# Softmax of the first attention: the negated maximum is added by VectorE from a broadcast tile instead of by a fourth product of TensorE

## What is computed

```python
q = _rmsnorm(hidden_states @ Wq_a, q_a_ln_w) @ Wq_b          # 32 heads, 128 + 64 wide
ckv = hidden_states @ Wkv_a
compressed, k_pe = (ckv[..., :KV_RANK], ckv[..., KV_RANK:])   # 64 and 64 wide
kv = _rmsnorm(compressed, kv_a_ln_w) @ Wkv_b
...
scores = jnp.einsum('bhqd,bhkd->bhqk', qf, kf) * scale
scores = jnp.where(causal, scores, jnp.finfo(scores.dtype).min)
probs = jax.nn.softmax(scores, axis=-1)
o = jnp.einsum('bhqk,bhkd->bhqd', probs, v)
return o.transpose(0, 2, 1, 3).reshape(b, s, H * VD) @ Wo
```

## Time and profile before

| | |
|---|---|
| three executions | 2632.04, 2634.44, 2639.09 us |
| profiled execution | 2627.89 us, its span 2626.1 us |
| mean granted clock of TensorE | 0.918 |
| TensorE busy, 12704 matmuls | 2225.0 us, 85% |
| VectorE busy | 1402.9 us, 53% |
| ScalarE busy | 1264.4 us, 48% |
| GpSimd busy | 629.5 us, 24% |
| stage of the 32 heads | about 205 to 858 us |

### The profile page before, as it was taken

How to read it: one execution, slowest core, us unless ns; L and a number is a source line. 1 busy time by engine, 2 the same in 40 slices (tenths; PEclk the granted TensorE clock), 3 DMA queues, 4 the chain that set the end, 5 groups by cost and what they waited for, 6 DMA issues and landing times. The chain is left out here.

```text
span 2626.1 us, 34151 instructions
## 1 busy us (share of the span) xinstructions
PE 2225.0 (85%) x12704; PEld 1310.7 (50%) x12704; DVE 1402.9 (53%) x1949; ACT 1264.4 (48%) x2113; POOL 629.5 (24%) x460
## 2 busy tenths in 40 slices
PE   4989999999999767759999957679999977998847
PEld 3657777777777653324444323234444333443434
DVE  3564555554554254559999654159999631113163
ACT  4545556655565232218888832118888841101330
POOL 1555555665566022400000022100000020001021
PEclk8989999999999888869999958879999998999868
DMA  4870111111110310331121001341121003000000
GB/s 102 260 223 25 53 52 52 56 44 52 52 53 32 109 35 21 107 68 20 20 38 20 2 17 53 125 70 23 28 48 28 2 17 129 0 0 5 14 27 34
DMA packets 78947, 138.97 MB, mean 53 GB/s; under 512 B 30808, under 2 KB 40792, under 8 KB 78832
## 3 DMA queue, kind: packets, MB, share of 16 engines
q1 hardware_dynamic: 78832, 137.40, 18.8%
HBM read 95.95 MB, written 41.03 MB: 52 GB/s over the span
## 5 line engine op out<-in xcount | busy, mean ns | idle before, releaser
L2159 POOL TENSOR_TENSOR l0a_p_low<-yT,l0a_p_high 128x1024 fp32r<-128x1024 f32 (+7 forms) x256 | 385.8, 1535 | 282.6 <-ACT l0a_p_high L2187 282.6
L173 POOL TENSOR_TENSOR applied<-prepared,neghalf 128x2 f32<-128x2 f32 x64 | 58.3, 911 | 1410.6 <-DVE prepared L154 1410.6
L1441 DVE TENSOR_REDUCE l2a_mx<-ps 128x2 f32<-128x1024 f32 x256 | 309.2, 1223 | 78.2 <-PE ps L1315 77.5
L1441 DVE TENSOR_REDUCE l1a_mx<-ps 128x2 f32<-128x1024 f32 x256 | 309.3, 1223 | 51.3 <-PE ps L1315 50.6
L2220 DVE TENSOR_REDUCE l0a_mx<-ps 128x1 f32<-128x512 f32 (+3 forms) x384 | 203.6, 554 | 235.9 <-PE ps L2066 145.0
L1422 ACT ACTIVATE l1a_prob<-ps 128x512 f32<-128x512 f32 x512 | 278.1, 596 | 75.2 <-PE ps L1343 58.6
L1422 ACT ACTIVATE l2a_prob<-ps 128x512 f32<-128x512 f32 x512 | 278.1, 596 | 68.6 <-PE ps L1343 50.6
L2176 ACT ACTIVATE yT<-ps 128x1024 f32<-128x1024 f32 (+7 forms) x256 | 166.2, 649 | 188.4 <-PE ps L2088 125.6
L2187 ACT CAST l0a_p_high<-yT 128x1024 fp32r<-128x1024 f32 (+7 forms) x256 | 172.7, 674 | 7.1
L191 ACT ACTIVATE f<-f,applied 128x512 f32<-128x512 f32 x64 | 48.6, 806 | 250.3 <-POOL applied L176 250.0
L1358 PE MATMUL ps<-l1a_prob,l1a_vext 128*32 128x256 f32 x2048 | 166.4, 405 | 0.0
(11 more groups left out here) (297 smaller groups left out, 4065.3 us busy)
## 6 DMA issues: line engine op xcount, KB each, us to landing
l0a_q<-l0a_q SPq DMA_DIRECT2D x32, 512.0 KB, 3.2
l0q_woh<-in_l0a_wo SPq DMA_DIRECT2D x16, 512.0 KB, 5.3
l0a_q<-f SPq DMA_DIRECT2D x32, 256.0 KB, 4.7
l0a_q<-l0q_q_pe SPq DMA_DIRECT2D x32, 256.0 KB, 3.5
l0a_recip_rows<-l0a_recip_row SPq DMA_DIRECT2D x32, 256.0 KB, 3.3
l0a_o<-l0a_o_pair SPq DMA_DIRECT2D x16, 512.0 KB, 2.8
yT<-l0a_o SPq DMA_DIRECT2D x16, 512.0 KB, 3.2
l1a_q<-l1a_q_parts SPq DMA_DIRECT2D x16, 256.0 KB, 5.3
```

The lines of the kernel that those rows point to most:

```text
L1441: nc.vector.tensor_reduce(mx[:, u % 2, :, p, t, c], banks(("pair", m)), AX.X, ALU.max).then_inc(s_red, 1)
L2159: nc.gpsimd.tensor_tensor(p_low[:, j % 4, P * j:T], prob[:, j % 4, P * j:T], p_high[:, j % 4, P * j:T], ALU.subtract).then_inc(s_pl, 1)
```

## The change

- `mrow`, `ones` and `diag` and their memsets and load are gone, and with them the fourth product of each part (L2086) and VectorE's multiply (L2225). `mcol` is 8 columns of fp32r instead of 128 of float32.
- `max_turn` makes eight products of 128 columns instead of one transpose: the weights are one column of `mcol`, broadcast to 128, and the moving operand is the identity; so every partition gets the negated maxima of all 1024 queries (`MAXIMA`, banks 6 and 7).
- ScalarE copies them to the tile `mrows` (128x1024, two buffers), behind step 4's cast. Chunk 0 of the head after waits for this copy.
- VectorE adds `mrows` to each score tile (`less_max`) and writes `prob`; ScalarE's exp reads and writes `prob`. TensorE waits for the addition of tile j (`s_less`) where it waited for the exp. The addition waits for its tile in PSUM, and for `p_high` and `p_low` of the tile that had the slot, which the exp's wait was before.
- VectorE's program is written anew, in steps like TensorE's: `invert` is in step 1, `negate` in step 2, `rest` in step 4, `finish` in step 5, and the additions stand between the reductions. In step 7 tile 1 of the next head is added before chunks 0 to 2 are reduced.
- On SyncE each `load` of a q comes after a `spread` instead of before it.

```diff
@@ -1725,11 +1725,10 @@
         def sb(n, shape, dt=F32):
             return mem.enter_context(nc.sbuf_tensor("l0a_" + n, shape, dt))
         self.q_high, self.q_low = sb("q_high", [P, 2, T], F32R), sb("q_low", [P, 2, T], F32R)
-        self.unit, self.mask, self.ones = sb("unit", [P, P], F32R), sb("mask", [P, P], F32R), sb("ones", [P, P], F32R)
+        self.unit, self.mask = sb("unit", [P, P], F32R), sb("mask", [P, P], F32R)
         self.c_high, self.c_low = sb("c_high", [P, NT, self.CV], F32R), sb("c_low", [P, NT, self.CV], F32R)
-        self.mrow = sb("mrow", [P, 2, T], F32R)
-        self.mx, self.mcol = sb("mx", [P, NT, 2]), sb("mcol0", [P, P])
-        self.diag = sb("diag", [NT, NT, P])
+        self.mrows = sb("mrows", [P, 2, T])
+        self.mx, self.mcol = sb("mx", [P, NT, 2]), sb("mcol0", [P, NT], F32R)
         self.mask16 = sb("mask16", [P, P], BF16)
 
 
...
     ST = [ps[:, 0:2, :].rearrange("p b n -> p (b n)"), ps[:, 2:4, :].rearrange("p b n -> p (b n)")]
     O = ps[:, 4:6, :].rearrange("p b n -> p (b n)")
+    MAXIMA = ps[:, 6:8, :].rearrange("p b n -> p (b n)")
     s_ph, s_pl = (chip.sem("l0h_" + n) for n in ("exps_high", "exps_low"))
     NH = MLA_HEADS
     OV = O[0:CV, :]
+
+    PLAN = [(3, 4, 5, 6), (6, 7, 8, 9), (9, 10, 11, 12)]
+    AHEAD = 3
 
     def bank(par, n):
         return ps[:, 6 + (par + n) % 2, :]
@@ -2025,15 +2023,15 @@
 
             load(2, 0, True)
             load(3, 1, True)
+            spread(0)
             load(4, 0)
-            spread(0)
             with sp.Fori(0, NH // 2 - 3) as i:
+                spread(i * 2 + 1)
                 load(i * 2 + 5, 1)
-                spread(i * 2 + 1)
+                spread(i * 2 + 2, i)
                 load(i * 2 + 6, 0)
-                spread(i * 2 + 2, i)
+            spread(NH - 5)
             load(NH - 1, 1)
-            spread(NH - 5)
             for h in range(NH - 4, NH):
                 spread(h, None if h % 2 else h // 2 - 1)
 
@@ -2052,12 +2050,9 @@
                     if not ready:
                         pe.wait_ge(s_high, h - 1)
                     if not first:
-                        pe.wait_ge(s_red, h * NMAX)
-                elif n == 1:
-                    if not first:
 
                         pe.wait_ge(s_mrow, h)
-                else:
+                elif n >= 2:
                     pe.wait_ge(s_red, h * NMAX + n - 1)
                 mm = nc.tensor.matmul(b[:, 0:width], q_high[:, par, qt * P:(qt + 1) * P],
                                       k_high[:, 512 * c:512 * c + width],
@@ -2068,22 +2063,22 @@
 
             def max_turn(h, par):
                 pe.wait_ge(s_neg, h + 1)
-                nc.tensor.transpose(bank(par, NMAX)[:, 0:P], mcol[:], chip.ident[:]).then_inc(s_mt, 1)
+                for t in range(NT):
+                    mm = nc.tensor.matmul(MAXIMA[:, t * P:(t + 1) * P], mcol[:, t:t + 1].broadcast_to([P, P]), unit[:],
+                                          start=True, stop=True)
+                mm.then_inc(s_mt, 1)
 
             def scores(h, par, j, ready=False):
 
-                if j == 0:
-                    pe.wait_ge(s_mrow, h + 1)
-                    if not ready:
-                        pe.wait_ge(s_low, h - 1)
+                if j == 0 and not ready:
+                    pe.wait_ge(s_low, h - 1)
                 for lo, hi in spans(j):
                     out = ST[j % 2][:, lo:hi]
                     diagonal = lo == P * j
                     keys = slice(j * P, (j + 1) * P)
                     nc.tensor.matmul(out, k_high[:, keys], q_high[:, par, lo:hi], start=True, stop=False)
                     nc.tensor.matmul(out, k_high[:, keys], q_low[:, par, lo:hi], start=False, stop=False)
-                    nc.tensor.matmul(out, k_low[:, keys], q_high[:, par, lo:hi], start=False, stop=False)
-                    mm = nc.tensor.matmul(out, ones[:], mrow[:, par, lo:hi], start=False, stop=not diagonal)
+                    mm = nc.tensor.matmul(out, k_low[:, keys], q_high[:, par, lo:hi], start=False, stop=not diagonal)
                     if diagonal:
                         mm = nc.tensor.matmul(ST[j % 2][:, lo:lo + P], mask[:], unit[:], start=False, stop=True)
                 mm.then_inc(s_st, 1)
@@ -2098,13 +2093,11 @@
                 mm.then_inc(s_pv, 1)
 
 
-            PLAN = [(3, 4, 5, 6), (6, 7, 8, 9), (9, 10, 11, 12)] + [(NMAX,) * 4] * 4
-            AHEAD = 3
             TURN_STEP = 3
 
             def head(h, par, first=False, last=False, no_second=False):
                 def chunks(j, part):
-                    if j < NT - 1 and not last:
+                    if j < len(PLAN) and not last:
                         for n in range(PLAN[j][part], PLAN[j][part + 1]):
                             max_chunk(h + 1, 1 - par, n)
                     if j == NT - 1 and not no_second:
@@ -2116,7 +2109,7 @@
                     if j == 0 and not first:
                         pv(h - 1, NT - 1)
 
-                    pe.wait_ge(s_exp, h * NT + j + 1)
+                    pe.wait_ge(s_less, h * NT + j + 1)
                     if j + 2 < NT:
                         scores(h, par, j + 2)
                     elif not last:
@@ -2167,13 +2160,14 @@
                 act.wait_ge(s_q[par], turn * 16 + 16)
                 nc.scalar.copy(q_high[:, par, :], q32[:, par, :]).then_inc(s_high, 1)
 
-            def head(h, par, next_turn, first, second=False):
+            def maxima(h, par):
+                act.wait_ge(s_mt, h + 1)
+                nc.scalar.copy(mrows[:, par, :], MAXIMA).then_inc(s_mrow, 1)
+
+            def head(h, par, next_turn, first, second=False, last=False):
                 for j in range(NT):
-                    act.wait_ge(s_st, h * NT + j + 1)
-                    if not (first and j < 4):
-
-                        act.wait_ge(s_pl, h * NT + j - 3)
-                    nc.scalar.activation(prob[:, j % 4, P * j:T], ST[j % 2][:, P * j:T], ACT.Exp,
+                    act.wait_ge(s_less, h * NT + j + 1)
+                    nc.scalar.activation(prob[:, j % 4, P * j:T], prob[:, j % 4, P * j:T], ACT.Exp,
                                          scale=SCALE).then_inc(s_exp, 1)
                     if j == 0 and not first:
                         if not second:
@@ -2185,6 +2179,8 @@
 
                         act.wait_ge(s_pv, h * NT + j - 3)
                     nc.scalar.copy(p_high[:, j % 4, P * j:T], prob[:, j % 4, P * j:T]).then_inc(s_ph, 1)
+                    if j == 4 and not last:
+                        maxima(h + 1, 1 - par)
                 if next_turn is not None:
 
                     cast(par, next_turn)
@@ -2194,13 +2190,14 @@
                 act.wait_ge(s_pv, h * NT + NT)
                 nc.scalar.copy(osum[:], O[0:KV_RANK + 1, :]).then_inc(s_os, 1)
 
+            maxima(0, 0)
             head(0, 0, 1, True)
             head(1, 1, 1, False, second=True)
             with act.Fori(1, NH // 2 - 1) as i:
                 head(i * 2, 0, i + 1, False)
                 head(i * 2 + 1, 1, i + 1, False)
             head(NH - 2, 0, None, False)
-            head(NH - 1, 1, None, False)
+            head(NH - 1, 1, None, False, last=True)
             act.wait_ge(s_on, NH - 1)
             lift(NH - 1)
 
@@ -2211,20 +2208,26 @@
                 nc.vector.tensor_tensor(q_low[:, par, :], q32[:, par, :], q_high[:, par, :],
                                         ALU.subtract).then_inc(s_low, 1)
 
-            def prepare(h, par, done=None):
-
-                for n, (qt, c, width, _) in enumerate(MAX_CHUNKS):
-                    if n == 6 and done is not None:
-                        invert(done)
-                    dve.wait_ge(s_mm, h * NMAX + n + 1)
-                    nc.vector.tensor_reduce(mx[:, qt, c:c + 1], bank(par, n)[:, 0:width], AX.X,
-                                            ALU.max).then_inc(s_red, 1)
+            def reduce_chunk(h, par, n):
+                qt, c, width, _ = MAX_CHUNKS[n]
+                dve.wait_ge(s_mm, h * NMAX + n + 1)
+                nc.vector.tensor_reduce(mx[:, qt, c:c + 1], bank(par, n)[:, 0:width], AX.X, ALU.max).then_inc(s_red, 1)
+
+            def negate(h):
                 dve.wait_ge(s_red, h * NMAX + NMAX)
-                nc.vector.tensor_reduce(mcol[:, 0:NT], mx[:], AX.X, ALU.max, negate=True).then_inc(s_neg, 1)
-                dve.wait_ge(s_mt, h + 1)
-                nc.vector.tensor_tensor(mrow[0:NT, par, :].rearrange("r (t q) -> r t q", t=NT),
-                                        bank(par, NMAX)[0:NT, 0:P].unsqueeze(1).broadcast_to([NT, NT, P]), diag[:],
-                                        ALU.mult).then_inc(s_mrow, 1)
+                nc.vector.tensor_reduce(mcol[:], mx[:], AX.X, ALU.max, negate=True).then_inc(s_neg, 1)
+
+            def less_max(h, par, j, first=False):
+
+                dve.wait_ge(s_st, h * NT + j + 1)
+                if j == 0:
+                    dve.wait_ge(s_mrow, h + 1)
+                if not (first and j < 4):
+
```

(64 more changed lines are left out.)

15 lines of the change are left out of this document (5 added, 10 removed).

## The result

The kernel after took 2661.38 us, the median of 5 runs (2654.84 to 2664.64); the kernel before took 2638.74 beside it (5 runs, 2632.04 to 2639.09). The ratio is 1.0087, with a 95% interval from 1.0066 to 1.0108: slower, by 0.9%. The profiled execution took 2661.96, with a span of 2659.9. In what follows one execution is out of line: one of e2's ten took 3053.44 us at a mean granted clock of 0.685, and e2's interval leaves it out.

A forecast was written before the change was run, and what follows sets the result against it. TensorE was the bound by busy sums, but waits on other engines were to decide: stretches 4.67 + 15.94 = 20.61 us per head against 20.33, +8.4 us over 30 heads, added to the median 2634.4 for 2643 us; range 2608 to 2672.

The forecast's parts named there:

- the waits eat what the products give: Main forecast: new TensorE waits on VectorE cancel the saved products, 0.28 us more per head, 2643 us; chance 0.50.
- The forecast's own range: 2631 to 2653 us, from other costs of the turn's products and overlapping VectorE starts.
- A: Stretch from the end of pv(h-1,7) to pv(h,0): two chains end together, so it stays 4.67 us.
- B: The rest of a head's period, from pv(h,0) to the end of pv(h,7): 15.66 us becomes 15.94.
- The twelve products: Fourth products removed from TensorE: 2.2 us per head, of which 0.35 + 0.35 lie in A.
- The baseline at the end of tile 1's products: In B, issue of tile 1's products ends 13.71 us after pv(h,0) before the change, 13.15 after it.
- Behind it: After tile 1's products: chunk 2 at 1.63 us, chunk 3 at 2.05, pv(h,7) ends at 2.79, against 1.95 before.
- The sum: A plus B: 20.61 us per head against 20.33, 0.28 more in 30 heads, +8.4 us.
- The port rival: VectorE's q_low shut out by GpSimd's SBUF reads: tile 0's products wait 0.7 us, +21 us, 2664 us; chance 0.20.
- The fast rivals: TensorE's sum at 2590 us, chance 0.07, and a partial gain of 0.3 to 0.9 us per head, 2616, chance 0.20.
- TensorE's sum: Rival: all waits covered, TensorE's busy time decides, 1.4 us per head off, 45 us, 2590 us; chance 0.07.
- What would show it: Signs: period 20.4 to 20.8 us, TensorE busy 25 to 45 us less, reduction waits about 2 us per head.

The follow-up runs named there:

- e2: e1 plus chunk 4 reduced before tile 2's addition in step 0: 2628.62 us, ratio 0.9962.
- e8: Kernel after, with only ScalarE's cast of tile 0 moved ahead of the copy of the sums: 2650.78 us, ratio 1.0067.
- e3: e2 plus ScalarE's cast of tile 0 ahead of its copy of the previous head's sums: 2600.73 us, ratio 0.9864.
- e6: e3 with the turn's eight products made twice into the same banks: 2626.25 us, ratio 0.9971.
- e9: e4 plus ScalarE's cast of tile 0 ahead of the copy of the sums: 2570.07 us, ratio 0.9737.
- e5: Kernel before, with only ScalarE's cast of tile 0 moved ahead of the copy of the sums: 2631.06 us, ratio 0.9984.
- e4: Kernel before without the fourth product, maxima made but never subtracted: 2590.71 us, ratio 0.983.
- e1: Kernel after, with chunks 0 and 1 reduced before tile 1's addition in VectorE's step 7: 2627.89 us, ratio 0.9972.
- e7: e3 with the turn in TensorE's step 4 instead of 3 and the maxima's copy behind step 5's cast: 2580.37 us, ratio 0.9806.
- e10: Kernel after, with VectorE's q_low held until tile 6's exp is made, so GpSimd starts first: 2692.53 us, ratio 1.0199.

## Why the prediction was right, and which step of it failed

The case that I forecast is the one that came: the waits eat what the products give. That the time fell into the range says less. The forecast's own range, 2631 to 2653, misses 2661.38, and the port's 2664 lies nearer to it than the forecast's 2643. The stated range held because it was made wide enough for a rival that did not come, which is luck; what decides for the forecast are the waits, point by point:

**A stays as it was: right.** From the first product behind pv(h-1,7) to pv(h,0) it was 4.84 (516.31 to 521.15) and is 4.85 (527.54 to 532.39). Chunk 6 starts 3.20 after tile 2's first product, predicted 3.09. That two chains end together is shown by three runs and not only argued: e2 shortens one and e8 the other, each for nothing, and e3 shortens both, for 0.77 per head.

**B up to the turn: right.** From pv(h,0): chunk 11 at 4.16 (predicted 4.16), the turn at 5.61 (5.61), pv(h,2) at 6.55 (6.49). The turn's products take 0.94 from the first to what follows (0.88 predicted), 0.12 each, and 0.11 each by e6.

**The twelve products: right**, 2.09 of 2.2 us by e9 (2.03 against e5), 1.32 of them outside A by e4 (I had 1.5, less 0.18 lost at the turn).

**The baseline at the end of tile 1's products is the step that failed**, where I wrote that it "ends at 13.15, now at 13.71 (514.53 in the head before", and that what comes behind it "is 1.95 now". It ends at 13.35 in the kernel after (545.74 less 532.39). Heads of the two parities aren't alike: 20.31 and 20.50 us. I took 514.53 from a head of 20.48 us, whose pv starts at 500.67, and subtracted its distance to the next pv(h,0), 6.62, from the 20.33 of the other parity. The timeline of the kernel before has the start of that head, and the same place in the head that starts at 521.15:

```profile
500.67 0.40 PE L2096 MATMUL ps<-l0a_p_high,l0a_c_high 128*66 128x512 f32 x1
...
535.02 0.22 PE L2062 MATMUL ps<-l0a_k_high,l0a_q_high 128*128 128x128 f32 x1
...
536.63 0.22 PE L2096 MATMUL ps<-l0a_p_low,l0a_c_high 128*66 128x128 f32 x1
```

The products end 13.86 behind the pv of the one head (514.53 less 500.67) and 13.87 behind that of the other (535.02 less 521.15), never 13.71. The 1.95 is right for the first head, but in the head that I walked it is 1.83 (535.02 to 536.85). Up to the end of tile 1's products 13.87 becomes 13.35: 0.52 less, where I had 0.56.

**Behind it: right.** Chunk 2 at +1.70 (predicted 1.63), chunk 3 at +2.04 (2.05), the end of pv(h,7) at +2.78 (2.79). Against 1.83 that is 0.95 lost per head, not 0.84. e1 takes it away and gets 0.97.

**The sum.** 0.28 was predicted, and 0.49 came as the mean of the two parities. In the head that I walked it is 0.43 (20.76 against 20.33): of the 0.15 that were missing, 0.12 is the 1.95 for 1.83, the rest the 0.56 for 0.52. In the heads of the other parity it is 0.54 or so: chunk 3 starts 2.18 behind tile 1's products there, not 2.04 (524.78 to 526.96 in TensorE's timeline of the kernel after). I walked one parity only. So +8.4 us was said, and 12.3 measured between the copies, 31 distances. The last two of these are 1.2 us shorter in after (18.75 and 14.73, against 19.25 and 15.46), where I had put nothing.

The medians differ by 22.6, and the profiled executions by 34. Of the 18.4 between 2643 and 2661.38, 4.3 are the median of before, 2638.74 here and 2634.44 in the prediction, 3.9 the 12.3 for 8.4, and some 10 lie outside the copies. The profiled executions show what such time can be. Before the first copy that of after is 4.8 us late (235.63 against 230.86), but e8, which starts with the same instructions, has its first copy at 230.41, so the change doesn't cause it. And in the third attention (its tiles are named l2a), where its maxima are made, TensorE's clock is low for longer. In both kernels it falls to 0.50 behind a stretch in which TensorE had gaps (busy 4.1 us from 1751.8 to 1757.8 before, and 4.1 from 1771.5 to 1777.5 after). Windows of the kernel before:

```profile
1770.00:1776.00 6.00, 5.73 (x38) 1.85 (x36) 3.60 (x4) 3.62 (x8) 0.00 (x0) 0.59 0.01 3
1776.00:1782.00 6.00, 5.79 (x59) 2.36 (x51) 5.68 (x6) 4.74 (x10) 0.00 (x0) 1.00 0.01 1
```

and of the kernel after, where the same work lies 19 us later:

```profile
1789.00:1795.00 6.00, 5.59 (x28) 2.17 (x30) 3.60 (x3) 3.84 (x8) 0.00 (x0) 0.50 0.00 0
...
1819.00:1825.00 6.00, 5.33 (x40) 2.09 (x40) 3.77 (x4) 3.48 (x8) 0.00 (x0) 0.76 0.00 1
```

The granted clock is back at 1.00 (2.4 GHz) from 1776 us before; in after it stays at 0.50 (1.2 GHz) until past 1819, with TensorE busy in nearly all of it. The stretch is about 27 us longer, and from the first to the last product for that attention's maxima (L1315) it is 376.9 us against 365.2. It doesn't come with the change each time: of the kernels made from after, the profiled executions of e1 and e2 have the low clock there for 37.5 and 44.4 us, those of e3 and e7 for 17.1 and 20.5, and before has 17.1.

The other four runs of after left no trace, but the mean granted clock of each is on record: 0.911 to 0.915 in the five of after, 0.914 to 0.920 in the four of e8, which has the same period and a median 10.6 us lower. In the runs of before beside the experiments the time goes with that clock too: five at 0.914 have a median of 2641.30 us, eight at 0.919 or 0.920 one of 2629.31. So a good part of the 10 us outside the copies goes with the clock of those executions. How much is not settled: e8 is 15.4 us above its runs of before, where its copies show 11.5 (637.87 less 626.34), and every kernel made from after has a median above what its copies give, from 1.4 us (e7) to 12 (e10), while those made from before (e4, e5, e9) are 0.5 above at most. A few us outside the copies may be the change's, and that stays open.

**The port rival didn't come, and exists.** q_low takes 1.21 us in after and TensorE waits for none:

```profile
L2208 DVE TENSOR_TENSOR l0a_q_low<-l0a_q,l0a_q_high 128x1024 fp32r<-128x1024 f32 x30 | 36.5, 1215 | 0.0
```

It starts 0.25 us ahead of GpSimd (540.95, against 541.20 in GpSimd's timeline); the walk said 0.3. GpSimd pays instead: its subtraction 384 columns wide takes 1.85 there, not 1.02, and ends 0.89 behind q_low. e10 moves q_low behind it and the period grows by 1.12, by 33.7 us between the copies (672.37 less 638.68); I had priced the rival at +0.7 per head. All of it stands at tile 0's products, as TensorE's timeline in e10 shows:

```profile
532.99 0.39 PE L2091 MATMUL ps<-l0a_p_low,l0a_c_high 128*66 128x512 f32 x1
534.28 0.47 PE L2079 MATMUL ps<-l0a_q_high,l0a_k_high 128*128 128x512 f32 x1 [0.91 <-DVE l0a_q_low L2208]
```

From start to start it is 1.29 here and 0.23 in after (542.14 to 542.37), so 1.06 more, and the next product comes 0.31 behind instead of 0.24. What stands behind q_low on VectorE adds nothing: the final multiply takes 1.44 in e10 (at 534.37) and 1.84 in after. The Trainium skill, page "SBUF — State Buffer", section "Who interferes with whom", has it that VectorE with two SBUF inputs and a GpSimd instruction that reads SBUF shut each other out, and that whoever issues first keeps the port. Both orders are now seen in the traces: 1.21 against 1.85, and 1.78 against 1.02.

The final multiply has both operands in SBUF too, and I overlooked that it meets GpSimd in the kernel before already, once for each parity:

```profile
507.49 1.02 POOL L2159 TENSOR_TENSOR l0a_p_low<-yT,l0a_p_high 128x384 fp32r<-128x384 f32 x1 [0.31 <-ACT l0a_p_high L2187]
508.12 1.47 DVE L2239 TENSOR_TENSOR l0a_o_pair<-l0a_osum,l0a_recip_rows 64x1024 f32<-64x1024 f32 x1
...
527.97 2.60 POOL L2159 TENSOR_TENSOR l0a_p_low<-yT,l0a_p_high 128x384 fp32r<-128x384 f32 x1 [0.32 <-ACT l0a_p_high L2187]
528.50 1.20 DVE L2239 TENSOR_TENSOR l0a_o_pair<-l0a_osum,l0a_recip_rows 64x1024 f32<-64x1024 f32 x1
```

In the first head GpSimd is ahead and the multiply ends 1.08 behind it. In the second GpSimd starts 0.53 ahead, and yet it is the one that grows, and ends 0.88 behind the multiply. Taken by the starts in the timeline, the page's rule fails there, and the measurement decides: who starts first doesn't always keep the port. What was issued first the trace doesn't show. In after the multiply takes 1.84, and that costs TensorE nothing: tile 1's addition, two instructions later, still waits 0.54 us for its products (546.10). The additions, with one operand in PSUM, never grew: 1.225 us at 1024 columns, 0.284 at 128, beside a GpSimd that works 413 of the stage's 665 us.

**The fast rivals are refuted for this order of VectorE.** TensorE's sum (2590) needs all waits covered; after has 2.1 us of them per head. But e3 and e7 show that the rival named the right resource: with three places of the order changed (e3) the changed kernel is 35 us below before, with the turn moved too (e7) 55.

**What would show it**, as listed: TensorE is busy 18.35 us of a head's 20.89 (439.31 of 500), before 19.61 of 20.40 (480.59 of 500), so 1.25 less and 39 us in 31 heads (25 to 45 said), its waits on reductions are 2.1 per head in two places (about 2), from copy to pv(h,0) it is 4.59 (4.6), VectorE is busy 469 us (470), the clock is 1.00. That TensorE would stay over 90% busy was wrong: it is 88%, at the clock of 1.00 all the same. The period was to be 20.4 to 20.8 and is 20.89, just outside.

## What to carry to other kernels

Work taken from the engine with the largest sum is worth only what of it lies outside the chains that end with it; walk one whole period in order of time, take every number of a difference from the same period, and where two parities differ walk both. Where work moves to an engine that runs in order, what it costs is set by what stands behind it in the queue: the additions fit by their sum, and one of them placed before the reductions that TensorE wanted turned a gain of 0.48 us per head (e1) into a loss of 0.49. And a range that holds only because a rival's price was put into it bears out no forecast: look for the row that tells the two apart. When one edit moves a wait and the time stands still, look for the second chain that ends at the same place and shorten both.
